# Gram products of the last two tiles as single samples in column quarters, with half layers between them and low-part signals in pieces

## The reference

```python
e = jnp.stack([tbl_0[ids[:, 0]], ..., tbl_26[ids[:, 26]]], axis=1)   # 512 x 27 x 128
dot = jnp.einsum('bnd,bmd->bnm', e, e)                               # Gram matrix of each sample
z = dot.reshape(512, 27 * 27)[:, [i * 27 + j for j in range(1, 27) for i in range(j)]]
h = jnp.concatenate([z, dense_ctx], axis=1)                          # 512 x 367
h = jnp.maximum(h @ W_top1 + b_top1, 0.0)                            # 512
h = jnp.maximum(h @ W_top2 + b_top2, 0.0)                            # 256
y = h @ W_top3
```

## Time and profile before

| what | value |
|---|---|
| median of 3 runs | 106.79 us (106.44 to 106.99) |
| profiled execution | 106.66 us, span 104.8 us |
| PE busy | 99.6 us, 95% of the span |
| weight loads (PEld) | 86.4 us, 82% |
| DVE, ACT, POOL busy | 79.5, 71.5, 62.1 us |
| granted TensorE clock, mean | 1.000 |

### The profile page before, as it was taken

How to read it: one execution, slowest core, us unless ns; L and a number is a source line. 1 busy time by engine, 2 the same in 40 slices (tenths; PEclk the granted TensorE clock), 3 DMA queues, 4 the chain that set the end, 5 groups by cost and what they waited for, 6 DMA issues and landing times.

```text
span 104.8 us, 2680 instructions
## 1 busy us (share of the span) xinstructions
PE 99.6 (95%) x1012; PEld 86.4 (82%) x1012; DVE 79.5 (76%) x240; ACT 71.5 (68%) x151; POOL 62.1 (59%) x68
## 2 busy tenths in 40 slices
PE   5989997999999999999999998999999988999992
PEld 5858785888888888888887797999999978999980
DVE  5599999999999899998969949996259540952212
ACT  4486999599896999969796359893358431961240
POOL 3777777777887777777777777777777300000000
DMA  2887998978849767589922222322222200000000
GB/s 54 237 195 221 195 222 177 229 184 189 199 102 245 176 167 170 117 236 327 353 74 53 55 58 53 85 68 59 73 53 59 68 6 0 6 12 12 6 1 0
DMA packets 5541, 12.57 MB, mean 120 GB/s; under 512 B 2066, under 2 KB 2804, under 8 KB 5401
## 3 DMA queue, kind: packets, MB, share of 16 engines
q1 hardware_dynamic: 3585, 8.44, 30.2%
q0 software_dynamic: 1920, 3.94, 16.0%
q10 hardware_dynamic: 24, 0.02, 0.1%
HBM read 12.15 MB, written 0.00 MB: 116 GB/s over the span
## 4 chain that ended last, share of the span: by engine, by line
PE 77%; DVE 7%; DMA 5%; ACT 4%; issue 2%; SPq 2%; DVEq 0%
PE acc L408 19%; PE acc L400 17%; PE gram_ps L438 12%; PE acc L456 11%; PE tr_ps L372 6%; PE acc L476 5%; DMA table<-in_tbl 5%; PE gram_ps L456 3%; DVE onehot L579 3%; DVE pairs L532 2%; PE gram_ps L381 2%; PE tr_ps L476 2%; DVE lo L585 2%; ACT embT L636 1%; SPq L295 1%
## 5 line engine op out<-in xcount | busy, mean ns | idle before, releaser
L358 POOL DMA_INDIRECT emb<-in_tbl,ids_sb x60 | 61.3, 1021 | 19.4 <-issue 18.0
L579 DVE TENSOR_SCALAR onehot<-idrel 125x512 fp32r<-125x512 f32 x90 | 32.1, 425 | 1.8 <-ACT idrel L650 1.8
L400 PE MATMUL acc<-onehot,hi 125*128 125x512 f32 x102 | 26.3, 400 | 0.2 <-DVE onehot L579 0.2
L408 PE MATMUL acc<-onehot,lo 125*128 125x512 f32 x102 | 25.7, 393 | 0.8 <-DVE lo L585 0.8
L408 PEld LDWEIGHTS acc<-onehot,lo 125*128 125x128 f32 x102 | 18.8, 188 | 5.9 <-DVE lo L585 2.1
L400 PEld LDWEIGHTS acc<-onehot,hi 125*128 125x128 f32 x102 | 18.6, 188 | 4.1 <-issue 0.3
L532 DVE COPY pairs<-gram_ps 26x96 f32<-26x96 f32 (+1 forms) x64 | 16.5, 258 | 7.1 <-PE gram_ps L438 5.8
L532 ACT COPY pairs<-gram_ps 26x96 f32<-26x96 f32 (+1 forms) x64 | 15.2, 238 | 7.5 <-PE gram_ps L438 6.1
L585 DVE TENSOR_TENSOR lo<-table,hi 125x256 fp32r<-125x256 f32 x51 | 18.1, 412 | 0.0
L636 ACT COPY embT<-acc 128x512 f32<-128x512 f32 (+2 forms) x13 | 13.4, 1048 | 6.8 <-PE acc L408 6.7
L438 PEld LDWEIGHTS gram_ps<-embT 128*58 128x58 f32 x512 | 14.2, 133 | 2.3 <-issue 1.8
(11 more groups left out here) (48 smaller groups left out, 56.2 us busy)
## 6 DMA issues: line engine op xcount, KB each, us to landing
table<-in_tbl SPq DMA_DIRECT2D x8, 480.0 KB
table<-in_tbl SPq DMA_DIRECT2D x3, 600.0 KB
w_sb<-in_W SPq DMA_DIRECT2D x1, 1024.0 KB, 8.2
emb<-in_tbl,ids_sb POOLq DMA_INDIRECT x60
w_sb<-in_W SPq DMA_DIRECT2D x1, 512.0 KB, 9.4
table<-in_tbl SPq DMA_DIRECT2D x2, 240.0 KB
pairs<-pairs SPq DMA_DIRECT2D x16, 15.0 KB
table<-in_tbl SPq DMA_DIRECT2D x8, 20.0 KB
```

What stands on the lines that cost most here:

```text
L358: pool.indirect_dma_start(emb[:, t % EMB_RING, gathered_features.index(f), :], None, tables[f], bass.IndirectOffsetOnAxis(ids_sb[:, t, f:f ...
L400: return nc.tensor.matmul(acc[:, b, 0:batch], hi[0:ROWS_K, b, c, :], one_hot(k, c), start=(c == 0), stop=False)
L408: return nc.tensor.matmul(acc[:, b, 0:batch], lo[0:ROWS_K, b, c, :], one_hot(k, c), start=False, stop=(c == CHS[k] - 1))
L579: nc.vector.tensor_scalar(one_hot(k, one), idrel[0:ROWS_K, b, 0:batch], float(one), None, ALU.is_equal).then_inc(onehot_by_dve, 1)
```

## The change

Three things. `lo_ready` is raised by every low instruction of DVE, and PE waits for it before every second chunk. `ABREAST` puts tiles 2 and 3 one sample to a matmul: 26 stationary columns, 26 moving ones, output in one of four quarters of the partitions. And `STEPS` is written anew: `tr(2, 0)` stands ahead of the first Gram products, each further turn one place earlier, and half a first layer (blocks 0 and 1, then 2 and 3) stands between the two units of tiles 2 and 3. The padding columns of tiles 2 and 3 need no zeros any more, so two memsets of DVE go.

```diff
-    HALF = 2
+    ABREAST = [2, 2, 1, 1]
...
-        STEPS = tr(1, [3]) + [("gram", 0, 0), ("gram", 0, 1)] + tr(2, [0]) + [("gram", 1, 0)] + tr(2, [1]) + [("gram", 1, 1)]
-        STEPS += tr(2, [2]) + [("h1", 0, None)] + tr(2, [3]) + [("h2", 0, None), ("gram", 2, 0)] + tr(3, [0]) + [("gram", 2, 1)]
-        STEPS += [("h1", 1, None)] + tr(3, [1, 2]) + [("h2", 1, None)] + tr(3, [3])
+        STEPS = tr(1, [3]) + tr(2, [0]) + [("gram", 0, 0), ("gram", 0, 1)] + tr(2, [1]) + [("gram", 1, 0)] + tr(2, [2])
+        STEPS += [("gram", 1, 1), ("h1", 0, None)] + tr(2, [3]) + [("h2", 0, None), ("gram", 2, 0)] + tr(3, [0])
+        STEPS += [("h1 first half", 1, None), ("gram", 2, 1), ("h1 second half", 1, None)] + tr(3, [1, 2, 3]) + [("h2", 1, None)]
         t = TILES - 1
-        STEPS += [("gram", t, 0), ("gram", t, 1), ("h1", t - 1, None), ("h1 unmoved slot", t, None), ("h2", t - 1, None),
+        STEPS += [("gram", t, 0), ("h1 first half", t - 1, None), ("gram", t, 1), ("h1 second half", t - 1, None),
+                  ("h1 unmoved slot", t, None), ("h2", t - 1, None),
                   ("h1", t, None), ("y", t - 1, None), ("h2", t, None), ("y", t, None)]
+        H1_PARTS = {"h1": range(H1C), "h1 first half": range(H1C // 2), "h1 second half": range(H1C // 2, H1C)}
...
+        def pieces_to(k):
+            return sum(CHS[:k]) // 2
...
-                    sp.wait_ge(lo_ready, parts_to(k - RING + 1))
+                    sp.wait_ge(lo_ready, pieces_to(k - RING + 1))
...
-                    for n, part in enumerate(parts(k)):
-                        if c == part.start:
-                            pe.wait_ge(lo_ready, parts_to(k) + n + 1)
+                    if c % 2 == 0:
+                        pe.wait_ge(lo_ready, pieces_to(k) + c // 2 + 1)
...
+                many = ABREAST[t]
+                rows = QUAD * (many - 1) + COLS
                 for g in range(GROUPS):
-                    for s in range(0, SG, HALF):
+                    for s in range(0, SG, many):
                         p0 = SG * (GROUPS * n + g) + s
-                        last = nc.tensor.matmul(gram_ps[QUAD * s:QUAD * s + ROWS, n, PITCH * g:PITCH * g + WIDTH],
-                                                vectors[:, QUAD * p0:QUAD * p0 + ROWS], embT[:, t, p0:p0 + HALF, 1:FEATS],
+                        last = nc.tensor.matmul(gram_ps[QUAD * s:QUAD * s + rows, n, PITCH * g:PITCH * g + many * COLS],
+                                                vectors[:, QUAD * p0:QUAD * p0 + rows], embT[:, t, p0:p0 + many, 1:FEATS],
                                                 start=True, stop=True)
...
-                        last = nc.vector.tensor_tensor(lo[0:ROWS_K, b, two, :], table[0:ROWS_K, r, two, :],
-                                                       hi[0:ROWS_K, b, two, :], ALU.subtract)
-                    last.then_inc(lo_ready, 1)
+                        nc.vector.tensor_tensor(lo[0:ROWS_K, b, two, :], table[0:ROWS_K, r, two, :],
+                                                hi[0:ROWS_K, b, two, :], ALU.subtract).then_inc(lo_ready, 1)
...
-            for t in range(1, TILES):
+            for t in range(1, sum(n > 1 for n in ABREAST)):
                 nc.vector.memset(embT[:, t, :, FEATS:QUAD], 0.0).then_inc(pads_zeroed, 1)
```

More of the change, by code:

```diff
@@ L127, in build_tower @@
     COLS = FEATS - 1
-    WIDTH = HALF * COLS
-    ROWS = QUAD * (HALF - 1) + COLS
-    PITCH = HALF * QUAD
-    assert WIDTH <= PITCH and GROUPS * PITCH * 4 <= 2 * 2048
+    PITCH = 2 * QUAD
+    assert max(ABREAST) * COLS <= PITCH and GROUPS * PITCH * 4 <= 2 * 2048
     with ExitStack() as ctx:
@@ L425, in gram @@
                         pe.wait_ge(vectors_out, NK + 1)
-                    pe.wait_ge(pads_zeroed, t + 1)
+                    if ABREAST[t] > 1:
+                        pe.wait_ge(pads_zeroed, t + 1)
                     count = tr_index(t + 1, 0)
@@ L434, in gram, with h1 @@
                 vectors = embT[:, t, :, :].rearrange("d p f -> d (p f)")
+                many = ABREAST[t]
+                rows = QUAD * (many - 1) + COLS
                 for g in range(GROUPS):
-                    for s in range(0, SG, HALF):
+                    for s in range(0, SG, many):
                         p0 = SG * (GROUPS * n + g) + s
-                        last = nc.tensor.matmul(gram_ps[QUAD * s:QUAD * s + ROWS, n, PITCH * g:PITCH * g + WIDTH],
-                                                vectors[:, QUAD * p0:QUAD * p0 + ROWS], embT[:, t, p0:p0 + HALF, 1:FEATS],
+                        last = nc.tensor.matmul(gram_ps[QUAD * s:QUAD * s + rows, n, PITCH * g:PITCH * g + many * COLS],
+                                                vectors[:, QUAD * p0:QUAD * p0 + rows], embT[:, t, p0:p0 + many, 1:FEATS],
                                                 start=True, stop=True)
                 last.then_inc(gram_done, 1)
-            def h1(t, slots):
+            def h1(t, slots, parts_of_layer):
                 pe.wait_ge(pairs_by_dve, QUADS * UNITS * (t + 1))
@@ L447, in h1 @@
                 pe.wait_ge(w1_loaded, 16)
-                for n in range(H1C):
+                for n in parts_of_layer:
                     if 0 < t < LAST and n % 2 == 0:
@@ L516, in _ @@
                 elif kind == "h1 unmoved slot":
-                    h1(t, [UNMOVED])
-                elif kind == "h1":
-                    h1(t, range(UNMOVED) if t == LAST else [UNMOVED, *range(UNMOVED)])
+                    h1(t, [UNMOVED], range(H1C))
+                elif kind in H1_PARTS:
+                    h1(t, range(UNMOVED) if t == LAST else [UNMOVED, *range(UNMOVED)], H1_PARTS[kind])
                 elif kind == "h2":
@@ L528, in move_pairs @@
             for s in quarters:
-                col = COLS * (s % HALF) + QUADS * a + q - 2
+                col = COLS * (s % ABREAST[t]) + QUADS * a + q - 2
                 c0 = (P // SG) * s + GROUPS * n
@@ L607, in _ @@
                         move_pairs(nc.vector.tensor_copy, t, arg, q, (0, 1)).then_inc(pairs_by_dve, 1)
-                elif kind == "h1":
+                elif kind in ("h1", "h1 second half"):
                     dve.wait_ge(weights_loaded, 16 * 4)
@@ L689, in _ @@
                         move_pairs(nc.scalar.copy, t, arg, q, (2, 3)).then_inc(pairs_by_act, 1)
-                elif kind == "h1":
+                elif kind in ("h1", "h1 first half"):
                     act.wait_ge(weights_loaded, 16 * 4)
```

## The result

The changed kernel takes 108.56 us (median, 107.89 to 118.68) beside 106.62 us (106.38 to 106.99) for the kernel before in the same series: a ratio of 1.0144, 95% interval 1.0089 to 1.0199. It is 1.5 us slower, where I had forecast 0.95 us faster. All ratios in this document leave out executions that are more than 1.5% above the fastest of their kernel, here that of 118.68 us. The profiled execution took 108.25 us, 1.59 us more than that of before.

The account below looks back on a forecast made before the run. TensorE, busy 95% of 104.8 us, was taken as the bound. Tile 3 starting at 86.4 and its moved slots at 95.7 gain 0.95 us: span 103.85 plus 1.86 around it, 105.7 us, range 105.2 to 106.2.

Parts of the forecast that it names:

- the unit of quarters: Gram units of tiles 2 and 3: 128 matmuls 6.7 ns from start to start, 0.86 us a unit against 1.70.
- my bound from above: Same Gram units: 128 x 26.6 ns, 3.41 us, if TensorE can't start matmuls faster than it does now.
- the 1.3 us from which I had said that it decides: Length of a Gram unit of 128 matmuls: below it the change is faster, above it slower.
- no faster start rate: Gram units: TensorE hands over a load and matmul every 26.6 ns at best; unit 3.41 us, time 114 us; chance 0.10.
- two by two: Gram units: quarters overlap only in pairs, unit stays 1.70 us, moved slots at 97.4, time 107.4 us; chance 0.10.
- The signals: Lookup phase: signals on each low instruction take up to 1.5 us from the lookups, most of it slack later.
- The front, booked at zero: Start of the Gram phase: earlier `tr(2, 0)` and `h1(0)` gain nothing; tile 2 starts at 75.1 instead of 75.04.
- The gathers end this stage: Before tile 3: `tr(3, 3)` waits for the last gather until 84.0; tile 3 starts at 86.4 instead of 86.87.
- Tile 3: Last tile from 86.4: second unit at 89.46, unmoved slot at 93.0, moved slots at 95.7 instead of 96.69.
- The size of the order's part: Last tile with units of 1.70 us: half layer before the second unit, copies 2 x 0.85 us later, 107.4 us.

Follow-up runs that it names:

- halves: The changed kernel with all tiles two samples to a matmul again, keeping the new order and the signals on each low instruction; 107.21 us, ratio 1.006.
- quarters: The changed kernel with the steps back in the old order, keeping column quarters in tiles 2 and 3 and the new signals; 110.86 us, ratio 1.0371.
- tail: New signals, two samples to a matmul, old steps up to the last tile, new list for the last tile; 106.57 to 107.59 us, ratio 1.0037.
- piecewise: The kernel before plus only the signals on each low instruction; ratio 0.9899 the first time, 0.9941 when run again.
- one pass: The changed kernel with tiles 2 and 3's Gram products in one bfloat16 pass, half the instructions, less exact; 104.50 and 104.81 us, ratio 0.9816.
- the shift of 48: The changed kernel with 48 more TensorE instructions in the warm-up; 154.1 us beside 154.95 for the kernel before on a slow chip, ratio 0.9949.
- the narrow one: The changed kernel with tiles 2 and 3's Gram products cut to 13 by 13 columns; single execution of 118.43 us, with a long gather issue.
- four shifts: The changed kernel with 100 (three runs: 157.99, 156.11, 157.77 us) or 48 (one run: 154.1 us) more TensorE instructions in the warm-up, on slow chips.

## Why the prediction was wrong

**The step that failed is the unit of quarters: "four quarters give 6.7 ns from start to start ... A unit is then 128 x 6.7 = 0.86 us".** That quarters overlap was right, and the spacing between gaps, 8.5 ns, is not far off (it would be 1.1 us for a unit). What is wrong is to carry a spacing from the `y` products to units of 256 instructions. It did not even hold for the twelve: 7 ns is the distance within groups of three, the groups started 108 ns apart, and the 0.34 us of the earlier trace rows over twelve are 28 ns a matmul. Instructions come in blocks of 256, one in about 3.5 us, which is 27 ns for a load and a matmul (3.5 us by 128). That is my bound from above, 26.6 ns, but its reason was another: the sequencer does hand them over faster, for up to a block. The measured units, 2.13, 1.87, 1.86 and 1.52 us, lie beyond the 1.3 us from which I had said that it decides. Waits for a block are shown as the cause in tile 3 (0.77 and 0.43 us) and for 0.31 us in tile 2; the rest of tile 2's excess, above all four gaps of 0.25 to 0.28 us, has another cause that is not known. The rival "no faster start rate" gave 3.41 us for a unit and 114 us, far too much, because the layers between the units use few instructions and let the supply catch up. The kernel came out near the rival "two by two", but by another mechanism.

From the forecast of 0.95 us faster to 1.59 us slower it is 2.5 us: 1.0 us because tile 3 starts at 87.43 instead of 86.4, and 1.6 us because its moved slots follow 10.87 us behind instead of 9.3 (95.7 less 86.4). These two make 2.6, since the prediction's 0.95 is by its own times 0.99 (96.69 less 95.7).

**The signals**: shown. The waits of the earlier trace rows are gone and the lookups end 1.3 us earlier (59.39 to 58.08). That was not so each time: the last low product starts 1.0 to 1.3 us earlier than the 58.98 us of before in four of the traces without a long gather (changed kernel, halves, quarters, tail) and 0.3 to 0.4 us earlier in two (piecewise, one pass).

**The front, booked at zero**: right in sum, by a wait that I had priced too low. `h1(0)`, moved ahead, waits 1.4 us for moved rows; tile 2 starts at 75.16, forecast 75.1. That depends on the landing of those rows: in "halves", with the same steps so far, they were in place at 68.2 instead of 69.4 us, and tile 2 starts at 73.96.

**"The gathers end this stage", 86.4**: right where TensorE is in time. With halves tile 3 starts at 86.43 behind a wait for the gather, in one pass at 85.94. With quarters TensorE reached the eleven transposes at 83.7 (forecast 82.5 for the last three, so 81.6 for the first), because the two units of tile 2 together took 2.3 us more than the forecast 0.86 us each. And then I had missed a wait: `tr(3, 3)` goes to the buffer of `tr(3, 1)` and waits until ACT has copied it (the row at 85.19; 0.6 us from start to start instead of 0.1). Hence 87.43.

**Tile 3**: the structure holds (copies of 2.21 us, forecast 2.22, unmoved slot behind DVE's last copy, 2.87 us on to the moved slots, forecast 2.7), the sizes of the two units do not. First start to second unit 3.98 us instead of 3.06, and second unit to the start of its copies on DVE 1.76 instead of 1.21 us. The forecast of 9.3 us from first unit to moved slots became 10.87, worse than the 9.82 of before.

**The size of the order's part** I had worked out in the rival and not weighed in the forecast: with units of 1.70 us it costs 1.1 us in the tail. By my own sum (9.3 us at 0.86, and twice what a unit takes more) it only comes out even with the 9.82 us of before at units of 1.1 us, and that is what the shift of 48 measured: 9.82 us with units of 1.08 and 1.23. The end hung on the very number that was least known. And with units of 0.47 us the old order is still 0.4 us shorter from the first unit to the moved slots, so the runs show no unit length at which the new tail wins.

**Open**: the gaps of 0.2 to 0.3 us inside tile 2's units (75.97, 80.96) stand at no block's edge. They are there in the changed kernel, "quarters", the narrow one and once in the one-pass kernel, where POOL's gathers run beside them, and in none of the seven traces of late chips (four shifts, three one-pass runs), where POOL was idle by then; no run took the gathers away by itself. Also open is why the signals took 1.3 us off the lookups in some executions and 0.4 us in others, which goes with their gain of 1.0% once and 0.6% the other time, and where the gather issues of 10.1 us come from.

## What to carry to other kernels

Splitting one matmul into more and smaller ones also multiplies instructions: count them per stage (float32 takes four to a product), and compare a stage's time with what the instruction queue delivers, here 256 in about 3.5 us. To find such a stall, number TensorE's records, look for gaps that end with "issue" and lie a multiple of 256 apart, and lay them beside the instruction queue's packets. A spacing read from three instructions is a burst, not a rate. When a new order is there only to serve a faster part, price the order with the part at its old speed first; here the prediction had that price, 107.4 us, and the order alone measured 107.21, slower than before. And where some executions hold a stall of 10 us, as with the signals in pieces here, count them before calling 1% a gain.

## What the runs showed of the hardware

- TensorE starts matmuls on 26 columns in four column quarters every 8.5 to 8.8 ns in two float32 passes (8.1 to 8.2 ns at 13 columns) and every 7.5 ns in one bfloat16 pass (8.1 ns for 128 in a row), each with its load.
- TensorE's instructions arrive in packets of 16 KB. Over all runs, a stall at a block's edge ends 1.2 to 1.5 us after the packet's last byte.
- Stalls of 1.75, 2.50 and 2.73 us had the granted clock fall to 1.2 GHz for 3.4 us at their end or up to 1.4 us behind it; two of 1.97 and 2.18 us did not.
- On some chips the lookups are far slower, and every kernel took some 150 to 161 us, the one of before too. With 48 instructions ahead one low product started at 65.26 us, the next at 67.39 and the next at 70.17, with idle time that ends with "issue", and from 36 to 59 us no matmul ran while DVE stood idle for 32 us by the same word. The instruction queue brought no packet between 18.9 and 91.2 us, so these are no waits at a block's edge. From 110 us on the Gram phase ran as elsewhere. Nothing here tells why.
